# Cross-attention on raw context in one core's attention and routed FFN block: key scale and key deviation applied to scores and probabilities, two moves in VectorE's order

## What is computed

```
x   : (32, 100, 256)      ctx : (32, 361, 192)
x1  = layernorm(layernorm(x), ln1_g, ln1_b);   x2 = layernorm(ctx, ln2_g, ln2_b)
q, k, v = x1 @ Wq + bq,  x2 @ Wk + bk,  x2 @ Wv + bv        (width 256)
attn = softmax(q @ k.T / 16);   x = x + (attn @ v) @ Wo + bo
h = layernorm(x)
aff = softmax(h @ Wr + br) over 31 experts, the three largest are kept as gates
x = x + h + gelu(h @ ws1 + bs1) @ ws2 + bs2 + sum over the kept of gate * (gelu(h @ W1 + B1) @ W2 + B2)
```

## Time and profile before

| | us |
|---|---|
| median of 3 runs (519.04 to 521.75) | 519.08 |
| the profiled execution | 518.88 |
| its span, first to last instruction | 517.1 |
| first phase, 0 to about 255 | 255 |
| first to last maximum of the scores (32 batches, 31 intervals) | 202.2 |
| TensorE busy over the span | 465.7 (90%) |
| VectorE busy | 350.8 (68%) |
| GpSimd busy | 322.8 (62%) |
| ScalarE busy | 246.9 (48%) |

### The profile page before, as it was taken

One profiled execution on the slowest core, in us unless ns is written; L12 is line 12 of the kernel. 1 busy time (PEld: TensorE's weight loads), 2 busy tenths in 40 slices (PEclk: granted clock), 3 DMA queues, 4 the chain that ended last, 5 costly groups with the idle time before them and its releaser, 6 DMA issues.

```text
span 517.1 us, 13549 instructions
## 1 busy us (share of the span) xinstructions
PE 465.7 (90%) x3204; PEld 409.2 (79%) x3204; DVE 350.8 (68%) x1556; ACT 246.9 (48%) x821; POOL 322.8 (62%) x363
## 2 busy tenths in 40 slices
PE   1898889898888898888899999999999999999891
PEld 1787678687676777767798999989999999999891
DVE  4748788777868688657466766666666666661684
ACT  1355555646464565646344545545454545553220
POOL 6213756747567575657168888778888888885000
PEclk9989999989898999999999999999999999999997
DMA  7464766767565982569369999979888888875998
GB/s 240 125 194 125 250 207 194 237 187 231 191 200 181 324 291 94 168 208 320 97 122 189 187 186 189 185 132 145 136 138 138 135 138 137 138 116 83 332 349 305
DMA packets 80621, 97.53 MB, mean 189 GB/s; under 512 B 8689, under 2 KB 65298, under 8 KB 80546
## 3 DMA queue, kind: packets, MB, share of 16 engines
q1 hardware_dynamic: 60786, 70.79, 45.5%
q0 software_dynamic: 19472, 25.61, 29.3%
...
q10 hardware_dynamic: 288, 0.27, 0.2%
HBM read 54.91 MB, written 41.73 MB: 187 GB/s over the span
## 4 chain that ended last, share of the span: by engine, by line
PE 44%; DVE 7%; DMA 5%; SPq 4%; issue 3%; POOL 1%; ACT 1%; POOLq 0%; DVEq 0%
PE bank L1184 16%; PE bank L1195 15%; PE bank L1173 4%; DMA sum<-y_sb,token 3%; DMA w_all<-sum 2%; SPq L449 2%; SPq L450 1%; SPq L448 1%; POOL sum L557 1%; DVE w_all L732 1%; PE bank L1101 1%; DMA xt<-expert_rows_in 1%; PE bank L1085 1%; PE bank L1110 1%; PE bank L1051 1%
## 5 line engine op out<-in xcount | busy, mean ns | idle before, releaser
L557 POOL DMA_INDIRECT sum<-y_sb,token x105 | 169.8, 1617 | 48.6 <-issue 22.6
L643 ACT ACTIVATE up<-bank,b_all 128x128 f32<-128x128 f32 x260 | 81.4, 363 | 103.5 <-PE bank L1184 66.5
L1184 PE MATMUL bank<-xtt,w1b 128*128 128x128 f32 x840 | 111.2, 275 | 1.1 <-DVE w1b L913 0.8
L1195 PE MATMUL bank<-w_all,up 128*128 x420 | 108.6, 381 | 0.0
L1184 PEld LDWEIGHTS bank<-xtt,w1b 128*128 128x128 f32 x840 | 102.1, 192 | 1.7 <-ACT xtt L669 1.6
L921 DVE TENSOR_SCALAR y_sb<-bank,gate,inverse 128x256 f32<-128x256 f32 x105 | 57.1, 543 | 54.3 <-PE bank L1195 53.8
L535 POOL DMA_INDIRECT expert_rows_in<-xt,slot x75 | 74.6, 995 | 25.3 <-issue 25.0
L1195 PEld LDWEIGHTS bank<-w_all,up 128*128 128x128 f32 x420 | 71.7, 191 | 5.6
L913 DVE COPY w1b<-w_all 128x512 f32 x105 | 46.9, 447 | 18.2 <-PE bank L1184 8.0
L669 ACT ACTIVATE xtt<-bank 128x256 f32<-128x256 f32 x105 | 40.1, 383 | 38.3 <-PE bank L1173 37.7
L1173 PE MATMUL bank<-ident,xt 128*128 128x128 f32 x210 | 40.1, 273 | 0.2 <-DMA xt<-expert_rows_in 0.2
(11 more groups left out here) (180 smaller groups left out, 938.3 us busy)
## 6 DMA issues: line engine op xcount, KB each, us to landing
xt<-expert_rows_in SPq DMA_DIRECT2D x105, 132.0 KB, 2.9
...
w_all<-in_ctx SPq DMA_DIRECT2D x32, 288.0 KB, 3.0
...
sum<-pad_rows SPq DMA_DIRECT2D x1, 3328.0 KB, 12.0
...
```

Source lines behind the costliest of these rows:

```text
L557: pool.indirect_dma_start(sums[s], bass.IndirectOffsetOnAxis(ap=token[sx][:, 0:1], axis=0), y_sb[sx][:, :], None, compute_op=ALU.add).then ...
L643: ins = act.activation(up[s][:, m * P:m * P + P], up_ps[s][:, m * P:m * P + P], ACT.Gelu, bias=b1_all[:, e, m:m + 1].rearrange("p o n -> p ...
L1184: mm = pe.matmul(up_ps[s][:, m * P:m * P + P], w[:, c * INTER + m * P:c * INTER + m * P + P], xtt[s][:, c * P:c * P + P], start=(c == 0), ...
L1195: mm = pe.matmul(down_ps[s], up[s][:, m * P:m * P + P], w, start=(m == 0), stop=(m == 1))
```

## The change

The context is no longer normalized. Let s be a key's standard deviation (with epsilon) and r its inverse. The folded key and value weights get ln2_g multiplied in and their mean over the 192 features taken out, so that the product with the raw context equals the product with the centred context. The bias column meets a value s in place of one. So a score is r times (the product with the raw context, s in the last row), and the mix takes probability times r against the raw context with s in its last column. In detail:

- `z`, its normalization on VectorE, the six transposes of it on TensorE and the two ScalarE copies go. The transposed context comes from DRAM (a second input, transposed on the host) as `ct` (96 partitions, twice 361 values, one batch in three buffers).
- GpSimd makes s twice, to `rs` and to the last column of the context tile `c_sb`. SyncE stores r and s of a batch to a DRAM tensor `key_rows` (256 pieces of 12 bytes), waits for that to land, and a step later loads r, spread to 100 partitions, to `rb` (144 KB) and s to the last row of `ct` (1444 bytes).
- VectorE: the maximum becomes one instruction that multiplies the scores by `rb`, writes them to `probs` and keeps the maximum, and a second that negates it. ScalarE's exponential reads `probs` in SBUF. The three copies of transposed probabilities take r as a scale; the two copies of the mix become one.
- The 192 features and the extra row are split 96 and 97 in place of 128 and 65. Keys are dealt to three groups by their number modulo 3, so that a partition's context is contiguous in DRAM; the transposes of the probabilities read every third column.
- VectorE's `step` begins with the new context's statistics, and the multiply and maximum stand ahead of `picks`.
- SyncE: the context comes at step b-3 in place of b-4, in six buffers, waiting for an older mix. Early expert weights are spread over 30 steps in place of 23, late ones of the second kind come in one piece of 2 MB at step 33.
- At the start: two more sums over the key weights and their centring ahead of the folds; the same for the value weights after step 0; value folds after step 1.

```diff
-D2B = D2 - P
-D2C = D2B + 1
-KT = [P, P, LK - 2 * P]
+H = D2 // 2
+D2C = H + 1
+KEYS = [len(range(k, LK, 3)) for k in range(3)]
...
+CS, CTS, RS = 6, 3, 6
...
             def load_ctx(b):
-                if b >= SLOTS:
-                    sp.wait_ge(ctx_norm, b + 1 - SLOTS)
+                if b >= CS:
+                    sp.wait_ge(mix_made, b + 1 - CS)
                     alone(sp)
...
+            def load_ct(b):
+                if b >= CTS:
+                    sp.wait_ge(scores_made, b + 1 - CTS)
+                    alone(sp)
+                sp.dma_start(ct[b % CTS][0:H, :, :], ctx_t[b].rearrange("(c p) j -> p c j", p=H)).then_inc(ct_in[b % CTS], 16)
+
+            def store_key_rows(b):
+                sp.wait_ge(ctx_std, 2 * b + 2)
+                alone(sp)
+                sp.dma_start(key_rows[b].rearrange("k (p t) -> p k t", t=3), rs[b % RS][:, 1:3, 0:3]).then_inc(key_rows_out, 16)
+
+            def load_key_rows(b):
+                sp.wait_ge(key_rows_out, 16 * (b + 1))
+                if b >= CTS:
+                    sp.wait_ge(max_made, b + 1 - CTS)
+                alone(sp)
+                sp.dma_start(rb[b % CTS][:, :], key_rows[b, 0, 0:LK].partition_broadcast(LQ)).then_inc(rb_in[b % CTS], 16)
+                sp.dma_start(ct[b % CTS][H:D2C, 1, :], key_rows[b, 1:2, 0:LK]).then_inc(ct_in[b % CTS], 16)
...
             def step(i):
-                if batch(i + 4) is not None:
-                    load_ctx(i + 4)
+                if batch(i + 3) is not None:
+                    load_ctx(i + 3)
                 if starts(i + 4) is not None:
                     load_x(starts(i + 4))
+                if batch(i + 1) is not None:
+                    load_ct(i + 1)
+                    load_key_rows(i + 1)
+                if batch(i + 2) is not None:
+                    store_key_rows(i + 2)
                 if i == FILL_STEP:
...
+                    pool.wait_ge(ctx_rstd, b + 1)
+                    pool.tensor_tensor(rs[r][:, 2, 0:3], rs[r][:, 0, 0:3], rs[r][:, 1, 0:3], ALU.mult).then_inc(ctx_std, 1)
+                    pool.tensor_tensor(c_sb[b % CS][:, :, D2], rs[r][:, 0, 0:3], rs[r][:, 1, 0:3], ALU.mult).then_inc(ctx_std, 1)
...
+                if new is not None:
+                    dve.wait_ge(c_in[new % CS], (new // CS + 1) * 16)
+                    for k in range(3):
+                        ins = dve.bn_stats(c6[new % 2][:, k, :], c_sb[new % CS][:, k, 0:D2])
+                    ins.then_inc(ctx_stat6, 1)
...
-                if met is not None:
-                    s, s4 = met % 2, met % SLOTS
-                    dve.wait_ge(ctx_rstd, met + 1)
-                    if met >= SLOTS:
-                        dve.wait_ge(mix_made, met + 1 - SLOTS)
-                    for k in range(3):
-                        ins = dve.tensor_scalar(z[s4][:, k, 0:D2], c_sb[s4][:, k, :], mv[s][:, k, 0:1],
-                                                rs[s][:, 1, k:k + 1], ALU.subtract, ALU.mult)
-                    ins.then_inc(ctx_norm, 1)
...
+                if rated is not None:
+                    s = rated % 2
+                    dve.wait_ge(scores_made, rated + 1)
+                    dve.wait_ge(rb_in[rated % CTS], (rated // CTS + 1) * 16)
+                    if rated >= 2:
+                        dve.wait_ge(probs_transposed, rated - 1)
+                    dve.tensor_tensor_reduce(probs[s][:, 0:LK], bank[s][0:LQ, 0:LK], rb[rated % CTS][:, :], 1.0, LOWEST, ALU.mult, ALU.max,
+                                             rowmax[s][:, 0:1]).then_inc(max_made, 1)
...
+            weights_with_bias(wk_aug, bk_s, 0).then_inc(aug_ready, 1)
```

263 lines of the change are left out of this document (121 added, 142 removed).

## The result

| | median us | lowest to highest | runs |
|---|---|---|---|
| before | 519.06 | 513.79 to 521.75 | 4 |
| after | 547.52 | 544.97 to 549.12 | 4 |

The ratio is 1.0593, 95% interval 1.0532 to 1.0653: 5.9% slower, 28 us, and outside the range of 507 to 533. The profiled execution of the changed kernel took 544.97 us with a span of 542.6, 25.5 us more than the span of before.

What follows compares the result with a forecast made beforehand. It took a ring between VectorE and TensorE to bound intervals of 6.5 us and TensorE those near 6.1. 518.9 - 10 (ordinary steps) + 13 (zeros) = 521.9, as a median 522.0 us, range 507 to 533.

Steps and rivals of the forecast that it cites:

- the ordinary steps: First-phase steps apart from the wait at the zeros: a gain of 10 us, bounds 3 to 19.
- The zeros: The 3328 KB transfer of zeros delays the context load of batch 28; VectorE stalls, costing 13 us (8 to 18).
- SyncE's round: From a VectorE step's start through scatters, products and issues to the context's landing: 12.0 to 13.5 us in two steps, nothing added.
- rival B: New transfers fill the steps, 5.4 to 6.4 us in a step of 6.2; no ordinary gain, 531 us; chance 0.17.
- TensorE's saved transposes: Six context transposes fewer save 0.64 us a step; 0.3 counted in intervals near 6.1 us, 0.8 in long ones.
- VectorE's ring: Loop between VectorE and TensorE in 6.5 us intervals: normalizations out, multiply and negation in, 0.34 us shorter.
- The wait ahead of `rinv`: Sign to look for: VectorE idle 1.3 us ahead of `rinv` in full steps.
- The order: VectorE's statistics first: up to 0.2 us in some steps; exponential 0.7 us earlier, useful only where TensorE waited for ScalarE's copies.
- GpSimd: Two more products make its full-step round 6.66 us; full steps gain about 0.15 us; idle time nearly gone in their runs.
- Strided transposes: TensorE's transposes of probabilities reading every third column: nothing taken, at worst 0.3 us a step.
- Rival C: Reads of every third column or small stores cost 0.5 us or more a step: 535 and over; chance 0.05.
- Start and end: Ahead of the first steps 0, within 2 us either way; at the end, with late weights in one piece, 0.

Runs made afterwards that it cites:

- the spread zeros: Changed kernel with the 3328 KB of zeros sent as 26 transfers over steps 4 to 29: 542.05 us, ratio 1.0459.
- the cheap store: Changed kernel with each batch's key rows stored as two pieces from a constant tile instead of 256 of 12 bytes: 532.55 us, ratio 1.0287.
- the kernel before with the store: Kernel before plus a store of 256 pieces of 12 bytes per batch, for which only the end waits: 519.08 us, ratio 1.0009.
- three causes gone: Changed kernel with key rows stored in four pieces of zeros, context four steps ahead, zeros spread over steps 4 to 29: 512.68 us, ratio 0.9888.
- idle transposes: Six unread transposes a step added: to the kernel with three causes gone 509.82 us, ratio 0.9818; to the changed kernel 549.95 us, ratio 1.0512.

## Why the prediction was wrong, point by point

The sum was 518.9 - 10 + 13. The second term was right in size. The first had the wrong sign: the ordinary steps lost 10.3 us.

**The zeros: right.** Forecast: load issued 13.3 us after the zeros, landed 19.7 after, wanted 6 after, a stall of 13 to 14, one interval of about 19 us. Measured: 14.6, 18.7, 5.0, a stall of 13.65, an interval of 19.37. The issues were held up longer (9.67 us in place of 7.57) and the load landed sooner, 4.09 us instead of 6.4. So the mechanism is as forecast, and that the stall fits so well is in part luck: an issue 1.3 us later, a landing 2.3 us shorter and a use 1 us earlier cancel. What the sum didn't have is that curing it gives only half back, since the 3.3 MB have to go somewhere (the spread zeros).

**The ordinary steps: the step that failed is "SyncE's round", and in it one term, the landing.** The prediction put 12.0 to 13.5 us into two steps, with 3.0 to 4.5 us for the landing, called it "as near to the limit as GpSimd is", and added nothing. The other terms held. In the round shown above VectorE's step began at 128.45 us and GpSimd's scatters ended at 133.54, 5.1 us (forecast 4.9); the four products took 1.8 (1.8) and the issues 2.0 (2.3). The landing measured 6.3 to 6.4 in the median.

```profile
128.45 0.88 DVE L715 BATCH_NORM_STATS2 c<-w_all 128x6 f32<-128x192 f32 x3 [0.93 <-DMA w_all<-in_ctx]
...
132.58 0.96 POOL L563 DMA_INDIRECT expert_rows_in<-xt,slot  x1 [0.30 <-issue]
```

So the round is 5.1 + 1.8 + 2.0 + 6.4 = 15.3, 7.65 us a step in a run of full steps; in the one shown it took 16.05. With gap steps between them the mean was 6.87. The runs show it from two sides: the load a step earlier gives 17.6 us back at an unchanged landing, and the cheap store gives 15 us back with a landing of 4.3.

The 3.0 was the landing at a share of 0.66. The prediction worked out the new share itself, in rival B: 5.4 to 6.4 us of all engines in a step of 6.2. Measured are 0.91 × 6.87 = 6.25 us. But it carried that number into B only, and left the landing in the main sum at the old kernel's value. One and the same quantity stood in the text with two values. The rows of before even had one landing in a busy stretch, 6.4 us at a share of 0.96. The share by itself would have led to 4.6 to 4.9, as the kernels with the cheap store show at 0.89 and 0.90; the rest is what the small pieces do to a load behind them, and that no row of before could show.

**Rival B happened, with too small a chance and too small a size.** Its upper end of 1.0 us for the pieces was near the mark (0.9 by the kernel before with the store, 1.1 by the share and steps of the cheap store: 6.25 less 0.81 × 6.40). It ended at "the steps gain nothing", 531, because its round of 6.6 us a step, 13.2 in two, leaves 4.2 us for the landing. What was measured in its place is 519 + 10 + 13 = 542, with 2.4 more from the start and the end. Its term for `rb`, 0.46 us at the old rate of 3.2 us a MB, was short as well: 0.78.

**TensorE's saved transposes: the gain does not exist by itself.** The prediction took 0.3 us of 0.64 a step, and 0.8 in the long intervals. In the kernel before, leaving five of the six out costs 0.8%: the granted clock goes down with the work. The Trainium skill, "TensorE: Matmul & The Clock Gate", in "Part 4: PE-mode transpose", says that a transpose doesn't count as busy for the clock in the way of other products; the time it gives beside it is of bf16. The float32 transposes here do: without them the granted clock is 0.87 in place of 0.95, with six idle ones 0.98 in place of 0.91. The measurement decides. Only together with the normalization did their removal bring anything, 15 us for both, where the sum had up to 19 as its high end; the normalization alone was not left out in any run. With the three causes gone the steps are 6.25 us long against 6.45 before, so without its three costs the change gives some 6 us and not 10, or 9 (ratio 0.9818) with idle transposes that keep the clock at 0.98.

**VectorE's ring.** The multiply with its maximum took 0.52 us, the low end; forecast 0.60 from two rows with a running sum. Its second part 0.08, the negation 0.15 (0.12). The ring is 0.08 less 0.03 shorter than forecast, which didn't matter, as VectorE waited 52.6 us for the context. The wait ahead of `rinv` is there as forecast, 0.9 to 1.6 us in many steps, 32 us over 20 steps against 31.5 over 22 before.

**The order.** "Worth something only where TensorE waited": in the kernel before the maximum ahead of `picks` gains 0.7%, both moves 0.9%, in the changed kernel nothing that can be told. The prediction had priced neither apart from the rest.

**GpSimd.** The two products took 0.19 and 0.20 us. It is what leads when the transfers don't (three causes gone, 6.25 us a step). In the changed kernel it isn't full in runs of full steps, against what the prediction gave as a sign.

**Strided transposes.** I had taken nothing, with 0.3 a step as the worst. Groups from 80 to 100 us, of the kernel before and of the one with three causes gone and idle transposes, both at the full clock in that window: count, busy us and mean ns of a weight load.

```profile
L1026 PEld LDWEIGHTS bank<-ident,w_all 100*128 100x128 f32 x6 | 0.7, 154 | 1.0 <-ACT w_all L608 0.8 <-issue 0.2
```

```profile
L1057 PEld LDWEIGHTS bank<-ident,w_all 100*120 100x120 f32 x6 | 1.2, 246 | 0.0
```

A weight load from every third column takes 0.25 us instead of 0.15, so three take 0.3 us more a step, the bound. Weight loads run beside products, and no run shows what this costs in time. Rival C asked for 0.5 us and over, and had both causes in one; the stores were the dear part, but not above their bound as it put it: they cost through the landing of the load behind them.

**Start and end.** Forecast 0 within 2 at the start and 0 at the end: measured +1.55 and +0.8.

**What stays open.** How much of the 28 us is clock: the changed kernel with idle transposes can't be told from it without. Why `rb`, which weighs as much in share as the small store, costs a third of it: the landings with and without small pieces ahead speak for the place in the queue, but no run moved the store behind the load in the changed kernel. Whether it matters for the time that `rb` runs on ten engines.
